# Moving a batch's softmax and its exponentials ahead of other work in a fused attention and quantized feed-forward kernel

## The reference

```python
def xattn(h, mem, mask):                       # h = layernorm(x)
    scores = einsum('bsd,bmd->bsm', h, mem) / sqrt(D)
    scores = where(mask, scores, -1e30)
    return einsum('bsm,bmd->bsd', softmax(scores), mem)

def linear_bit(x, w, g):                       # rmsnorm, rounding to 8 bits, ternary weights
    return einsum('bsd,od->bso', act_quant(rmsnorm(x, g)), ternary_quant(w))

x = x + xattn(layernorm(x), ctx, mask)
y = layernorm(x)
h = silu(linear_bit(y, w1, g1)) * linear_bit(y, w2, g2)    # width 2048
x = x + linear_bit(h, w3, g3)
```

## Time and profile before

| | |
|---|---|
| Time before, median of 3 runs | 445.47 us (444.27 to 445.84) |
| The profiled execution | 444.06 us |
| Its span, first to last instruction | 442.3 us |
| Mean granted TensorE clock | 0.954 of full speed |
| Busy: PE, DVE, POOL, ACT | 90%, 86%, 81%, 78% |
| Period of a batch in the loop | 48 us |

### The profile page before, as it was taken

The page is one execution under the profiler, slowest core; times in us unless marked ns, Lnnn a source line. Parts: engine busy times, 40 slices in busy tenths (PEclk is TensorE's granted clock), DMA queues, the critical chain, the costliest instruction groups (busy, mean ns, idle before and its releaser), DMA issues.

```text
span 442.3 us, 8289 instructions
## 1 busy us (share of the span) xinstructions
PE 398.4 (90%) x1870; PEld 179.0 (40%) x1870; DVE 382.3 (86%) x835; ACT 343.5 (78%) x618; POOL 358.3 (81%) x559
## 2 busy tenths in 40 slices
PE   8326596899999999999999999999999989999996
PEld 8102232334434443444344444444344443444443
DVE  5599598999799979997999979997999799798794
ACT  3677779687998789886998698878988697667661
POOL 0149888999889988898879987998889897899970
PEclk9755796999999999999999999999999999999999
DMA  6999881545675547843684568554784425354541
GB/s 256 398 333 367 282 189 24 143 90 125 171 194 103 119 105 188 184 103 81 170 194 92 117 168 189 105 119 102 183 185 103 88 66 113 80 96 101 106 103 73
DMA packets 110359, 66.40 MB, mean 150 GB/s; under 512 B 100736, under 2 KB 100864, under 8 KB 106752
## 3 DMA queue, kind: packets, MB, share of 16 engines
q1 hardware_dynamic: 110336, 66.14, 58.5%
HBM read 33.10 MB, written 8.39 MB: 94 GB/s over the span
## 4 chain that ended last, share of the span: by engine, by line
PE 53%; POOL 13%; DVE 12%; ACT 10%; issue 9%; DVEq 1%; DMA 1%; POOLq 0%; SPq 0%; ACTq 0%
PE S L1279 29%; PE DN L1312 15%; POOL stageB L549 5%; PE R L1258 3%; ACT stageB L740 3%; DVE stageB L972 3%; ACT prob L695 2%; DVE hm L978 2%; POOL c L538 2%; ACT L695 2%; PE DN L1320 1%; DVE ga L945 1%; PE R L1225 1%; ACT junk_x L718 1%; ACT sg L748 1%
## 5 line engine op out<-in xcount | busy, mean ns | idle before, releaser
L549 POOL TENSOR_TENSOR stageB<-stageB,g3b 128x512 f32<-128x512 f32 x127 | 161.9, 1289 | 7.4 <-DVE stageB L972 4.8
L1279 PE MATMUL S<-W2q,q12T 128*128 128x512 f16 x512 | 134.2, 385 | 5.3 <-DVE W2q L1044 3.3
L1279 PE MATMUL S<-W1q,q12T 128*128 128x512 f16 x512 | 135.9, 389 | 1.2 <-ACT sg L748 0.9
L1312 PE MATMUL DN<-W3q,stageB 128*128 128x512 f16 x496 | 122.2, 380 | 0.5 <-DVE W3q L1044 0.4
L748 ACT ACTIVATE sg<-S,asc 128x512 f32<-128x512 f32 x128 | 86.9, 682 | 25.5 <-PE S L1279 23.4
L972 DVE TENSOR_TENSOR stageB<-sg,S 128x512 f32<-128x512 f32 x128 | 86.1, 678 | 20.0 <-ACT sg L748 20.0
L978 DVE TENSOR_REDUCE hm<-stageB 128x1 f32<-128x512 f32 x127 | 85.9, 677 | 2.0 <-POOL stageB L549 1.9
L1279 PEld LDWEIGHTS S<-W2q,q12T 128*128 128x128 f16 x512 | 50.4, 99 | 69.4 <-DVE W2q L1044 4.5
L1279 PEld LDWEIGHTS S<-W1q,q12T 128*128 128x128 f16 x512 | 48.8, 100 | 70.2 <-issue 9.2
L1312 PEld LDWEIGHTS DN<-W3q,stageB 128*128 128x128 f16 x496 | 47.9, 98 | 59.1 <-issue 1.1
L755 ACT ACTIVATE junk<-stageB 128x1024 bf16<-128x1024 f32 x64 | 67.3, 1051 | 4.3 <-DVE stageB L972 4.2
(11 more groups left out here) (127 smaller groups left out, 431.1 us busy)
## 6 DMA issues: line engine op xcount, KB each, us to landing
X<-in_x SPq DMA_DIRECT2D x8, 1024.0 KB, 6.3
out_x<-X SPq DMA_DIRECT2D x32, 256.0 KB, 2.7
xTs<-in_xT SPq DMA_DIRECT2D x7, 1024.0 KB, 7.2
X<-in_w1T SPq DMA_DIRECT2D x4, 1024.0 KB, 10.7
stageB<-in_w2T SPq DMA_DIRECT2D x4, 1024.0 KB, 18.5
X<-in_w3T SPq DMA_DIRECT2D x4, 1024.0 KB, 9.2
ctxr<-in_ctx SPq DMA_DIRECT2D x16, 128.0 KB, 3.0
ctxc<-in_ctx SPq DMA_DIRECT2D x8, 128.0 KB, 4.4
```

Of the source, the lines that this page charges most:

```text
L549: nc.gpsimd.tensor_tensor(gh[q][:, part], hp[:, part], g3b[:, part], ALU.mult).then_inc(s_gh_made, 1)
L1279: mm = nc.tensor.matmul(bank[n % 2][:, :], q12T[q][:, i * KD + k, :], w[:, n, k, :], start=(k == 0), stop=(k == KD - 1))
L1312: mm = nc.tensor.matmul(bank[:, :], src[:, k, :], W3q[:, k, :], start=(k == 0), stop=(k == KH - 1))
```

## The change

Two calls are moved; no instruction is added, removed or altered. VectorE's `attention_softmax(b + 1)`, in slot j = 0 of batches 1 to 6, goes from behind gate 3 to ahead of gate 2. ScalarE's `attention_exp(b + 1)`, in slot j = 1 of the same batches, goes from behind the square of the last tile's second half to ahead of it.

```diff
@@ ScalarE's slot
                 silu(t, 0, j % NZ)
+                if attn and j == 1:
+                    attention_exp(b + 1)
                 square(t - 1, 1)
                 if attn and j == 0:
                     attention_ccT(b + 1)
-                if attn and j == 1:
-                    attention_exp(b + 1)
@@ VectorE's slot
                 gate(t, 1)
                 if attn and j < 3:
                     stage_a_max(t + 2, (j + 2) % NZ)
+                if attn and j == 0:
+                    attention_softmax(b + 1)
                 gate(t, 2)
                 worth_3(t - 2, j % 2)
                 if ahead and not (attn and j < 3):
@@
                 max_3(t, 0, j % 2)
                 result(t - 2)
                 gate(t, 3)
-                if attn and j == 0:
-                    attention_softmax(b + 1)
                 max_3(t, 1, j % 2)
```

## The result

The changed kernel takes 451.11 us (median of 4, 450.66 to 452.69) against 444.87 us for the kernel before in the same comparison (443.99 to 445.84). The ratio is 1.015, 95% interval 1.0124 to 1.0175: slower by about 6.2 us, beyond the 0.5% that can be told from no change. Forecast were 449.9 us and slower.

The account below looks back on a forecast made before the run. TensorE was taken as the bound, with 1.07 us idle a batch. 0.45 behind silu 1 plus 0.4 at the down projection gave 0.85 us a batch, +5.1 us over six: 449.9 us, range 445.0 to 453.5.

Parts of the forecast that it names:

- What bounds the kernel: TensorE, busy 46.93 of 48 us a batch; its idle 1.07 us is the wait for the exponentials ahead of the transposes.
- the three signs of being wrong: Second slots' wait for `anm` under 1 us, a table load starting ahead of it, or the transposing DMA landing in time.
- Part 1: Softmax ahead of gate 2: softmax 3.4 us sooner, VectorE's later work 0.85 us late, TensorE losing some 0.55 us.
- The middle that I took between the two ends: VectorE's last softmax step meeting GpSimd's `xrs`: silu 0 and all behind it 0 to 0.2 us later, 0.1 taken.
- Part 2: Exponentials ahead of the square: probabilities 1.9 us sooner, square 2.45 us late, silu 1 of tile 13 1.3 us late.
- My term of 0.45 us a batch: At the matmuls behind silu 1: TensorE 0.45 us later than before, the saved 1.07 us already counted.
- The transposing DMA: Tile 12's quantization 1.4 us late, against 0.55 us slack plus TensorE's own 0.45: 0.4 us stall at the down projection.
- The step that failed: After the down projection, ScalarE's and VectorE's remaining 1 us lateness fits their consumers' slack; next batch only 0.85 us late.
- (a): Only the first stall, DMA hidden: 0.35 to 0.45 us a batch or less, 445 to 448 us; chance 0.23.
- (b): Faster: second table load runs while ScalarE waits for `anm`, silu 1 on time, 441.7 us; chance 0.13.
- (c): GpSimd's 2.45 us not absorbed; tile 14's silus late, 0.5 us more a batch, 453; chance 0.09 together with the drain.
- The drain of 1.38 us: Moved table load behind a running silu also pays a drain: 8.3 us more, near 458; chance 0.09 together with (c).

Follow-up runs that it names:

- the fastest version: Changed kernel plus GpSimd's mean and quantization ahead of the root, result(t - 2) earlier in first slots, and an added GpSimd wait in slots 2 and 3: 438.77 us.
- the half-way runs: Each half of the change alone on the kernel before: softmax moved only, 445.4 us; exponentials moved only, 464.02 us.
- the reordered GpSimd queue: Changed kernel with GpSimd's mean of tile t + 2 and quantization of tile t + 1 ahead of the root in second slots: 443.19 us.
- the early result: result(t - 2) ahead of max_3(t, 0) in first slots, added to the changed kernel with mean and quantization ahead of the root: 443.67 us.

## Why the prediction came out as it did

**What bounds the kernel** was right: in the kernels before and after and in the fastest version the period is 46.7 to 46.8 us of TensorE's work plus its stalls. None of the three signs of being wrong came: the wait for `anm` is 1.72 us, the load stands behind it, and TensorE waits for the transposing DMA.

**Part 1** was right in kind and near in size. Forecast were a softmax 3.4 us sooner, 0.85 us more for all behind it and 0.55 us for DN; measured for DN are 0.42. The middle that I took between the two ends for VectorE's last step was on the wrong side: it took 0.43 us, and `xrs`, which starts 0.15 us behind it, went from 1.02 to 1.14. The step started first, so that GpSimd paid fits; at 0.12 us it is argued, not tested. The whole half, timed alone, costs 1.0 us net, just clear of the noise.

**Part 2** was right as a chain. In the frame of the earlier trace rows the square starts at 216.68 - 2.95 = 213.73 (forecast 213.75), the variance at 216.58 (216.9), silu 1 at 218.71 (219.0). The missing 0.3 us are in two terms: from the square's end to `anm` 1.40 us (the square ends with its read at 217.81, `anm` starts at 219.21), not 1.63, mostly since `hs` took 0.19 us where the earlier trace rows has 0.38; and 0.32, not 0.39, from `anm` to the variance. So silu 1 is 1.0 us late, not 1.3 or 1.4. TensorE's matmuls behind it stand at 222.40 - 2.95 = 219.45 against 219.46: the new stall eats the saved one exactly. My term of 0.45 us a batch was 0.0.

**The transposing DMA** was forecast at 0.4 us and cost 0.64. The quantization is 1.0 us late, less than the 1.4 assumed, but TensorE was not late by the 0.45 that I set against it. The slack was less, too: 0.36 us by these rows (1.00 us late at the issue, 0.64 at the matmuls), against the 0.55 that I read from issue plus 3.1 us.

**The step that failed** is the sentence "from there ScalarE's and VectorE's remaining lateness (about 1 us) is less than the slack of their consumers". VectorE's lateness against GpSimd changed which of them gets in first, in the third slot and then in the last. Each time the pair takes 1 us longer. Gate 1 of the last slot then comes too late, and that cost 0.42 us of stall (0.53 in the period). In the third slot of the changed kernel GpSimd idles 0.26 us for VectorE's `X` (L936) ahead of `anm`, which it doesn't in the kernel before, so VectorE is the late one there. I had the rule in hand, at the softmax, and didn't apply it to the slots behind.

So 0.85 us a batch was made of 0.45 + 0.4 where 0.0 + 0.64 + 0.42 was measured; the rest to 1.12 is spread in hundredths. Two misses of opposite sign kept the total near, and that is luck. The direction doesn't hang on it: the DMA's 0.64 us alone makes the batch longer, and the half-way runs and the reordered GpSimd queue bear out the chain from the square.

**The rivals.** (a), the DMA hidden, did not happen. (b), the faster one, needed a table load that runs while ScalarE waits for `anm`; the load stands behind the variance in both kernels. A gain can be had, though, in another way: once `anm` and the quantization don't wait for the square, the change brings 0.3%, and 1.3% with the collisions and the wait for DN removed too. (c) was right that lateness would cost once more further on, and near in price: 0.42 us a batch where it had 0.5. It had the wrong carrier and place, though: GpSimd's scales and the silus of tile 14, where it was VectorE's gate 1 of tile 15. The drain of 1.38 us beside a table load (the Trainium skill, ScalarE: Activation LUTs, "What ACT_TABLE_LOAD costs") is not there: the load behind a running silu starts 0.01 us behind it, at 214.04, and the first exponential stands 1.30 us after that, at 215.34.

## What to carry to other kernels

Work moved ahead of another on an in-order queue delays that other, and what counts is what stands behind its consumer on the next engine's queue: here one root of 128 values (`stage_h_root`) held the mean, the quantization and, through them, two more engines. Before giving up on such a reorder, reorder the consumer's queue as well. And account for stalls by the distance between starts, stall by stall, until they sum to the change of the period; a total that fits can hide a term too many and a term too few.

## What the runs showed of the hardware

Two VectorE instructions of 0.75 us each took 2.44 us as a pair when a GpSimd product of 1.3 us got in between, and 1.42 us otherwise. In the last slot a delay of VectorE of 0.7 us against GpSimd (0.13 to 0.83 us behind `aa`) went with the change from one to the other. With an added wait on GpSimd, which adds no work, the longest of these instructions took 754 ns instead of 1768, and the kernel, with GpSimd's new order and the early result in both versions, took 438.77 us instead of 443.67.
